# Fourier layers of a four-layer network: complex channel mixing by three real products instead of four, in nine chunks instead of five

## What is computed

```python
spec = jnp.fft.rfft2(x, axes=(2, 3), norm='ortho')      # 64 x 33 complex numbers a channel
# in four groups of 128 channels, at each frequency:
def cmul(ar, ai, w, b):
    or_ = ar @ w[0] - ai @ w[1] + b[0]
    oi_ = ai @ w[0] + ar @ w[1] + b[1]
    return (or_, oi_)
o1r, o1i = relu(cmul(xr, xi, w1, b1))                   # both parts
o2r, o2i = cmul(o1r, o1i, w2, b2)
y = jnp.fft.irfft2((o2r + 1j * o2i) * spec, s=(H, W), axes=(2, 3), norm='ortho')
```

## Time and profile before

| what | value |
|---|---|
| median of 3 runs | 5749.74 us (5747.33 to 5753.3) |
| profiled execution, its own time | 5756.4 us |
| its span | 5754.5 us |
| PE busy (matmul) | 5327.1 us, 93% |
| DVE busy | 3898.3 us, 68% |
| ACT busy | 2409.8 us, 42% |
| POOL busy | 2369.4 us, 41% |
| mean granted clock of TensorE | 0.973 |

### The profile page before, as it was taken

One profiled execution on the slowest core, in us unless ns is written; L12 is line 12 of the kernel. 1 busy time (PEld: TensorE's weight loads), 2 busy tenths in 40 slices (PEclk: granted clock), 3 DMA queues, 4 the chain that ended last, 5 costly groups with the idle time before them and its releaser, 6 DMA issues. The chain is left out here.

```text
span 5754.5 us, 139522 instructions
## 1 busy us (share of the span) xinstructions
PE 5327.1 (93%) x43062; PEld 3758.4 (65%) x43062; DVE 3898.3 (68%) x14034; ACT 2409.8 (42%) x6894; POOL 2369.4 (41%) x3910
## 2 busy tenths in 40 slices
PE   5999999999879999999999999997999996899999
PEld 2444444444358888888888888885666664577777
DVE  5666666656578888888888888875666666344444
ACT  0111111111046666666666666663333332333333
POOL 1444444444346555555565656651221221122221
PEclk8999999999979999999999999998999998899999
DMA  4434444334324444444444444442222211222221
GB/s 184 159 121 160 147 135 163 118 121 134 110 82 121 121 123 121 122 121 123 120 126 118 125 120 125 123 122 89 95 79 79 95 63 49 85 95 79 85 87 75
DMA packets 606260, 650.56 MB, mean 113 GB/s; under 512 B 176816, under 2 KB 506936, under 8 KB 594648
## 3 DMA queue, kind: packets, MB, share of 16 engines
q1 hardware_dynamic: 447624, 497.78, 27.4%
q10 hardware_dynamic: 157904, 144.22, 7.5%
HBM read 363.90 MB, written 278.00 MB: 112 GB/s over the span
## 5 line engine op out<-in xcount | busy, mean ns | idle before, releaser
L1496 PE MATMUL proj_ps<-proj_w_sb,proj_h 128*128 128x512 f32 x3072 | 1349.9, 597 | 0.0
L1496 PEld LDWEIGHTS proj_ps<-proj_w_sb,proj_h 128*128 128x128 f32 x3072 | 578.6, 191 | 747.1 <-issue 727.2
L1399 DVE SCALAR_TENSOR_TENSOR proj_lin<-proj_ps,proj_rstd,proj_wbias_sb 128x512 f32<-128x512 f32 x384 | 284.1, 747 | 496.8 <-PE proj_ps L1496 490.5
L1811 POOL TENSOR_TENSOR scan_b_step<-scan_core,scan_rate_last 128x128 f32<-128x128 f32 x512 | 324.8, 634 | 630.2 <-DVE scan_core L2071 630.2
L2280 PE MATMUL scan_ps_y<-scan_o_t,proj_wo_sb 128*128 128x128 f32 x4096 | 570.4, 283 | 2.1 <-ACT scan_o_t L1914 2.1
L2280 PEld LDWEIGHTS scan_ps_y<-scan_o_t,proj_wo_sb 128*128 128x128 f32 x4096 | 500.6, 193 | 32.8 <-ACT scan_o_t L1914 2.6
L1880 ACT ACTIVATE scan_square<-scan_ps_z 128x64 f32<-128x64 f32 x1024 | 219.0, 219 | 484.2 <-PE scan_ps_z L2199 469.7
L1308 POOL TENSOR_TENSOR proj_by_cos<-proj_lin,proj_rope 128x512 f32<-128x512 f32 x256 | 333.4, 1315 | 166.7 <-DVE proj_lin L1399 124.8
L1314 POOL TENSOR_TENSOR proj_gk<-proj_rec,proj_gain_sb 128x256 f32<-128x256 f32 x256 | 181.1, 728 | 532.3 <-DVE proj_rec L1420 532.3
L266 POOL TENSOR_TENSOR fourier_spec<-fourier_prod 128x448 f32<-128x448 f32 (+1 forms) x80 | 86.6, 1083 | 696.3 <-DVE fourier_prod L410 696.3
L2211 PE MATMUL scan_ps_w<-scan_step,scan_record 64*128 64x128 f32 x4088 | 358.0, 295 | 11.9 <-DVE scan_step L2076 11.7
(11 more groups left out here) (315 smaller groups left out, 12318.9 us busy)
## 6 DMA issues: line engine op xcount, KB each, us to landing
scan_record<-records SPq DMA_DIRECT2D x258, 392.0 KB
records<-proj_rec ACTq DMA_DIRECT2D x256, 392.0 KB, 3.8
spectra<-fourier_spec SPq DMA_DIRECT2D x16, 2112.0 KB, 6.4
fourier_spec<-spectra SPq DMA_DIRECT2D x16, 2112.0 KB, 8.2
proj_h<-x SPq DMA_DIRECT2D x32, 1024.0 KB, 6.7
queries<-proj_q ACTq DMA_DIRECT2D x128, 256.0 KB, 3.8
gradients<-scan_stored SPq DMA_DIRECT2D x512, 64.0 KB
scan_q_in<-queries SPq DMA_DIRECT2D x128, 256.0 KB, 7.7
```

Source lines behind the costliest of these rows:

```text
L1399: v.scalar_tensor_tensor(lin[q][:, n], ps[q][n][:], rstd[k][:, j:j + 1], T.wbias[:, n], ALU.mult, ALU.add).then_inc(lin_sb.sem, 1)
L1496: last = pe.matmul(ps[j % 2][n][:], h[k][:, ct, j * P:(j + 1) * P], T.w[:, n, ct], start=ct == 0, stop=ct == CT - 1)
L1811: v.tensor_tensor(b_step[g][:], core[g][:], rate_last[g][:, :, 2:3].broadcast_to([P, PB, HD]), ALU.mult).then_inc(b_step_sb[g].sem, 1)
```

## The change

Both Fourier functions change in the same way.

- A complex product is made of three real matmuls: with a shared product `once = w_re (a_re + a_im)`, the real part is `once - (w_re + w_im) a_im` and the imaginary part `once + (w_im - w_re) a_re`. Each mixing step then has three matmuls, each alone in its part of PSUM (no accumulation), in place of four.
- POOL adds real and imaginary parts ahead of each step: `xsum` (`sums`) for the first, `hsum` (`sum_hidden`) for the second. ACT copies the shared product from PSUM to SBUF (`copy_once1`, `copy_once2`). DVE adds it to both parts (`combine_hidden`, one instruction of two times the chunk's width; `combine_mixed`, two instructions with the bias). ACT's relus now read and write SBUF, in place.
- The gate by the spectrum was four DVE instructions out of PSUM. It becomes one DVE instruction of twice the width for the products with the real part (`times_re`), one of the same size on POOL for those with the imaginary part (`times_im`), and the same subtraction and addition on POOL.
- Nine chunks (six of 4 columns, 256 numbers; three of 3 columns, 192 numbers), one batch of rows after each of the first eight.
- All weights of a function are loaded once at its start, and POOL makes the negated sum and the difference once for each channel group.
- `fourier_forth` only: the block sums are spread out one by one (`box_of_last`): one after each column batch from the third on, three a chunk in the mixing phase, the small ones last. The scaling of the rows out of `psD` goes from DVE to ACT (`row`), and three of the four sums of squares go into the column phase.
- `fourier_back` only: the one-column correction `dc_added` comes after the second part of the scaling and not after the fifth.

```diff
-CHUNKS = [(0, 7), (7, 14), (14, 21), (21, 27), (27, 33)]
+CHUNKS = [(0, 4), (4, 8), (8, 12), (12, 16), (16, 20), (20, 24), (24, 27), (27, 30), (30, 33)]
@@ fourier_forth, gpsimd
+            def sum_hidden(u, q, c):
+                n = width(c)
+                pool.wait_ge(hidden_sb.sem, hidden_sb.at(u, c + 1))
+                if c >= 2:
+                    pool.wait_ge(mix2_ps.sem, mix2_ps.at(u, c - 1))
+                nc.gpsimd.tensor_tensor(hsum[q][:, 0:n], hidden[q][:, 0, 0:n], hidden[q][:, 1, 0:n], ALU.add).then_inc(hsum_sb.sem, 1)
+            def times_im(u, k, q, c):
+                pool.wait_ge(mixed_sb.sem, mixed_sb.at(u, c + 1))
...
+                nc.gpsimd.tensor_tensor(pv, mv, spec[k][:, s0:s1].rearrange("p s e h -> p e s h"), ALU.mult).then_inc(by_im_sb.sem, 1)
+            def gate(u, k, q, c, cf):
+                times_im(u, k, q, c)
+                pool.wait_ge(by_re_sb.sem, by_re_sb.at(u, c + 1))
+                pool.wait_ge(by_im_sb.sem, by_im_sb.at(u, c + 1))
...
+                nc.gpsimd.tensor_tensor(re, pv[:, 0, 0], pv[:, 1, 1], ALU.subtract)
+                nc.gpsimd.tensor_tensor(im, pv[:, 0, 1], pv[:, 1, 0], ALU.add).then_inc(prod_sb.sem, 1)
...
+                for c in range(NCH):
+                    sum_hidden(u, (k * NCH + c) % 2, c)
+                    if c:
+                        gate(u, k, (k * NCH + c - 1) % 2, c - 1, cf)
+                gate(u, k, (k * NCH + NCH - 1) % 2, NCH - 1, cf)
@@ fourier_forth, scalar: mixing phase
+                for c in range(2):
+                    copy_once1(u, c)
                     if not last:
-                        evacuate(u, ROW + 2 * c - 1)
...
+                        evacuate(u, ROW + c)
+                    relu(u, k, ct, c)
+                energy_of_last(u, 1 - k, 3)
+                for c in range(NCH):
+                    copy_once2(u, c)
+                    if not last and c < NB1:
+                        row(u, k, c)
+                        if c + 2 < NB1:
+                            evacuate(u, ROW + c + 2)
+                    if c + 2 < NCH:
+                        copy_once1(u, c + 2)
+                        relu(u, k, ct, c + 2)
@@ fourier_forth, vector
+            def combine_hidden(u, q, c):
+                n = width(c)
+                dve.wait_ge(once1_sb.sem, once1_sb.at(u, c + 1))
+                dve.wait_ge(mix1_ps.sem, mix1_ps.at(u, c + 1))
+                both = psA[1][:].rearrange("p (r n) -> p r n", r=2)[:, :, 0:n]
+                v.tensor_tensor(hidden[q][:, :, 0:n], both, once1[:, 0:n].unsqueeze(1).broadcast_to([P, 2, n]),
+                                ALU.add).then_inc(pre_sb.sem, 1)
+            def combine_mixed(u, q, c, adds):
+                n = width(c)
+                dve.wait_ge(once2_sb.sem, once2_sb.at(u, c + 1))
+                dve.wait_ge(by_im_sb.sem, by_im_sb.at(u, c - 1))
+                for r, add in enumerate(adds):
+                    done = v.scalar_tensor_tensor(mixed[q][:, r, 0:n], psB[1][:, r * CW:r * CW + n], add, once2[:, 0:n],
+                                                  ALU.add, ALU.add)
+                done.then_inc(mixed_sb.sem, 1)
+            def times_re(u, k, q, c):
...
+                dve.wait_ge(mixed_sb.sem, mixed_sb.at(u, c + 1))
+                dve.wait_ge(prod_sb.sem, prod_sb.at(u, c - 1))
...
+                v.tensor_tensor(pv, mv, spec[k][:, s0:s1].rearrange("p s e h -> p e s h"), ALU.mult).then_inc(by_re_sb.sem, 1)
...
+                for c in range(NCH):
                     q = (k * NCH + c) % 2
-                    dve.wait_ge(prod_sb.sem, prod_sb.at(u, c - 1))
...
+                    combine_mixed(u, q, c, (bias_re[k][:], bias[:, ct, 3:4]))
+                    few = 2 if c < NCH - 1 else NP - boxed
+                    for g in range(boxed, min(boxed + few, NP)):
+                        box_of_last(u, 1 - k, g)
+                    boxed = min(boxed + few, NP)
+                    times_re(u, k, q, c)
+                    if c + 2 < NCH:
+                        if boxed < NP:
+                            box_of_last(u, 1 - k, boxed)
+                            boxed += 1
+                        combine_hidden(u, (k * NCH + c) % 2, c + 2)
@@ fourier_forth, tensor
+                pe.matmul(psA[0][:, 0:n], wt[:, ct, 0], part_of(xsum, c), start=True, stop=True).then_inc(once1_ps.sem, 1)
+                pe.matmul(psA[1][:, 0:n], wneg[:, ct, 0], x[:, :, 1, :], start=True, stop=True)
+                pe.matmul(psA[1][:, CW:CW + n], wdif[:, ct, 0], x[:, :, 0, :], start=True, stop=True).then_inc(mix1_ps.sem, 1)
...
+                pe.wait_ge(hidden_sb.sem, hidden_sb.at(u, c + 1))
                 if c:
-                    pe.wait_ge(terms_sb.sem, terms_sb.at(u, c))
...
+                    pe.wait_ge(mixed_sb.sem, mixed_sb.at(u, c))
+                pe.matmul(psB[1][:, 0:n], wneg[:, ct, 1], hidden[q][:, 1, 0:n], start=True, stop=True)
+                pe.matmul(psB[1][:, CW:CW + n], wdif[:, ct, 1], hidden[q][:, 0, 0:n], start=True, stop=True)
+                pe.wait_ge(hsum_sb.sem, hsum_sb.at(u, c + 1))
+                pe.matmul(psB[0][:, 0:n], wt[:, ct, 2], hsum[q][:, 0:n], start=True, stop=True).then_inc(mix2_ps.sem, 1)
...
+                for c in range(2):
+                    mix1(u, k, ct, c)
+                    if not last:
+                        turn_rows(u, c, 1 - k)
                 for c in range(NCH):
-                    mix2(u, k, c)
...
+                    mix2(u, k, ct, c)
+                    if not last and c < NB1:
+                        transform_rows(u, c)
+                        if c + 2 < NB1:
+                            turn_rows(u, c + 2, 1 - k)
+                    if c + 2 < NCH:
+                        mix1(u, k, ct, c + 2)
@@ fourier_back, vector
+                for c in range(NCH):
                     q = (k * NCH + c) % 2
...
+                    combine_mixed(u, q, c, (bias_re[k][:], bias[:, ct, 3:4]))
+                    if c < NB1 and not first:
+                        row_back(u, it, k, c)
+                    times_re(u, k, q, c)
+                    if c + 2 < NCH:
+                        combine_hidden(u, q, c + 2)
```

More of the change, by code:

```diff
@@ L540, in unit @@
+            def unit(u, it, k, ct, last):
+                pe.wait_ge(row_sb.sem, row_sb.at(u, NB1))
                 turn_columns(u, 0)
@@ L746, in rows_back @@
[L746 to L758 removed]
+                    done = nc.scalar.activation(hidden[q][:, r, 0:n], hidden[q][:, r, 0:n], ACT.Relu, bias=bias[:, ct, r:r + 1])
@@ new lines, in relu, with row_back, unit @@
+                done.then_inc(hidden_sb.sem, 1)
+            def row_back(u, k, t):
+                evacuate(u, t, (k + t) % 2)
+            def unit(u, it, k, ct, first, final=False):
+                for c in range(2):
+                    copy_once1(u, c)
+                    if not first:
+                        row_back(u, k, c)
+                    relu(u, k, ct, c)
+                for c in range(NCH):
+                    copy_once2(u, c)
+                    if not first and c + 2 < NB1:
+                        row_back(u, k, c + 2)
+                    if c + 2 < NCH:
+                        copy_once1(u, c + 2)
+                        relu(u, k, ct, c + 2)
```

691 lines of the change are left out of this document (379 added, 312 removed).

## The result

| kernel | median us | ratio to before, 95% interval | profiled execution | its span |
|---|---|---|---|---|
| before | 5748.92 (5747.33 to 5753.30, 4 runs) | 1 | 5756.40 | 5754.5 |
| after | 5823.42 (5814.38 to 5824.51, 4 runs) | 1.0125 (1.0107 to 1.0142) | 5814.38 | 5812.4 |

A forecast was written before the change was run, and what follows sets the result against it. PE bounds the kernel before; after it, a loop over DVE and ACT. 15 x 3.8 + 9 - 15 x 0.6 + 8 = +65 us on 5756.4 gives 5821, as median 5815 us; range 5640 to 5900.

The forecast's parts named there:

- The chain, back: Mixing phase of `fourier_back`: DVE and ACT loop from end of `mixed` (M) to the next, 4.66 us; unit 50.7.
- The chain, forth: Mixing phase of `fourier_forth`: same loop from M (end of `mixed`) with block sums, first steps 6.1 us; unit 59.3.
- The sum: Whole kernel: 15 x 3.8 + 9 - 15 x 0.6 + 8 = +65 us on 5756.4.
- The edges: Last unit of forth 9 us more, first of back 8 more (0 to 15); weight loading up to 3 us.
- Rival 1: DVE and POOL don't collide at `times_re`: back's step 4.0 us, units 46.0 and 52.6, kernel 5630 us; chance 0.22.
- Rival 2: New stalls in forth let PE's clock fall to half: a step of 6.1 becomes 8, 5920 us; chance 0.08.
- Rival 3: The loop over DVE and ACT is 0.2 to 0.3 us a step shorter: 5740 to 5765 us; chance 0.08.
- Rival 4: Narrow products on PE cost more than their width: at most 0.3 us a unit, hidden; left out, no chance given.

The follow-up runs named there:

- e5: The changed kernel with `times_re` ahead of the copy out of `psD` on DVE, in `fourier_back` alone: 5768.6 us.
- e9: The changed kernel with ACT's `copy_once2` of the next chunk ahead of the relus instead of behind them, in both functions: 5681.4 us.
- e10: The changed kernel with `copy_once2` ahead of the relus, `times_re` first in back, spread block sums behind `combine_hidden` in forth, and no image loops: 5681.1 us.
- e4: The changed kernel with POOL's `times_im` waiting for DVE's `times_re` of the same chunk, in both functions: 5735.0 us.
- e6: The changed kernel, in forth alone with `times_re` and `combine_hidden` right behind `mixed`, block sums behind them and large ones spread: 5754.9 us.
- e3: The changed kernel with 25 of the 32 block sums of forth left out, so it computes less: 5656.0 us.
- e2_before_four: The kernel before with four units instead of two in its Fourier loop bodies, nothing else changed: 5761.5 us.

## Why the prediction was right, and where not

**The chain, back.** It came out term by term. From M = 5233.42: POOL ends at M + 1.35 (forecast 1.36), `times_re` at 1.90 (1.93), `combine_hidden` at 2.50 (2.56), the copy at 3.70 (3.74), the next `mixed` at 4.60 (4.66). Unit 50.6 (50.7). That it is the hold that makes 0.6 us of it, e5 shows; that it is a loop over DVE and ACT, e9 and e10.

**The chain, forth.** From M = 4513.94: the held block sum ends at M + 2.15 (2.21), `times_re` at 2.77 (2.82), `combine_hidden` at 3.90 (3.98), M again at 6.00 (6.1). Unit 58.9 (59.3). The place of PE's wait I had wrong in part: it isn't 2 us at `mix2` but 0.6 there and 1.0 at the next `mix1`, which waits for `combine_hidden`. POOL is busy 39.4 us of such a unit and not 35, since its own instructions are held as well. Two of the prediction's sums are 0.1 off (1.3 + 37.5 + 11.8 is 50.6 in back, 7.2 + 18.3 + 5.7 + 13.0 is 44.2 in forth); they cancel in the total.

**The sum, term by term**, in the profiled executions: forth 15 x 3.37 = +50.6 (forecast 57); back 15 x -0.69 = -10.4 (-9); last unit of forth with what follows until the next norm +8.7 (9); first unit of back +8.8 (8); head of forth +1.9 and the stages between -1.2 (0). That is +58, against 65. Then two things that the sum did not have:

- *The turns of the loops, +26.* The prediction went by units in the middle of a stage and never asked what a body of four units instead of two does at its turn. The step that failed is "The edges". It put the turns at nothing without a reason. The trace of before could have raised the question and given a first price: the pairs turned without any cost, but the scan's long body costs 2.5 to 3.4 us at each of its turns. Four such turns would have been some 12 us, an estimate from those gaps; the runs showed 26, since the gaps in back are twice as long and the clock falls behind all four.
- *The unchanged part, -26* in these two executions. The sum was added to the time of the profiled execution of before, which took the first 3.94 ms as fixed. What shortens it stays open.

Together 58 + 26 - 26 = +58 between the profiled executions (5814.4 - 5756.4), and +74.5 between the medians. That the forecast of 5815 lies within 9 us of the median is thus partly luck: two missing terms of opposite sign. The direction isn't: the mixing phases alone carry it.

**The rivals.** Rival 1 (no collision) is out: `times_re` 1.36 in the mean in back. Its units were close to what another order reached, though: with e9's order on ACT they are 46.0 and 54.3 (rival 1 said 46.0 and 52.6). Rival 2 (clock) is out for the units (1.00), and true only behind the turns and at the edges. Rival 3 (a shorter loop): the loop was 0.06 shorter in back and 0.1 in forth, not 0.2. Rival 4: widths cost what they should (256 wide 0.43).

**The expectations of single runs** were too large where I freed one resource and forgot the next one in line: in e4 it was POOL's `hsum`, in e5 the loop itself (4.0 without the hold), in e6 DVE's queue under three holds. In e3 it was too small, since the order of two starts changed with it.

## What to carry to other kernels

When one step is split over more engines, write the chain from the end of one step to the end of the next and mark which engines it closes over: here it closed over DVE and ACT, so TensorE's 3.8 and 5.3 us less of busy time a unit gave nothing in forth and 0.7 us in back, and moving one copy ahead of two relus on ACT gave 142 us. Cut such a loop before you tune what stands in it: with the loop cut, the two orders on DVE that had gained 50 and 66 us gained nothing more. Of two instructions of DVE and GpSimd that both read SBUF, put the one on the critical chain first; a hold of the other one costs nothing as long as no one on the chain waits for it. Look at a loop's turn as its own place in the program when its body grows.

## What was not expected of the hardware

- The turn of a loop with a body of 2200 or more PE records costs PE a gap of 6.5 to 7.1 us in `fourier_back`, 0.95 to 3.6 in `fourier_forth` and 2.5 to 3.4 in the scan; the long units of after and e2_before_four are 1.3 to 2.3 us longer than their gaps, with the clock at 0.50 behind them. With 1128 records there is no gap. Written out, the two Fourier functions have none of it.
- The unchanged projection and scan end at a time that goes with the rest of the program: the norm's matmul starts at 3909.7 to 3922.8 us in the seven kernels with the changed functions and loops, at 3927.7 to 3932.5 in the four without loops, at 3938.8 and 3936.1 in before and e2_before_four. One profiled execution each; the cause was not looked for. Parts of kernels are better compared from a common point inside the trace than by the whole.
- A DVE instruction of 16 numbers is held as long as one of 256 when it begins behind POOL's: 854 ns in the mean instead of 184.
